# Low parts of the weights divided anew between VectorE and GpSimd, the row shift on GpSimd, and new orders on five engines

## What is computed

```python
x = x + 0.5 * ffn(layernorm(x))
x = x + attention(layernorm(x))
x = x + 0.5 * ffn(layernorm(x))

def ffn(x):                    # w_gate, w_up: 1024 x 256; w_down: 256 x 1024
    return (silu(x @ w_gate.T) * (x @ w_up.T)) @ w_down.T

def attention(x):
    x = x / max(norm(x), 1e-12) * 16 * gamma
    q, k, v = split(x @ w_qkv)           # then rotary positions on q and k
    p = softmax(mask(q @ k.T / 8))
    return (p @ v) @ w_out
```

## Time and profile before

| | us |
|---|---|
| median of three runs | 587.42 |
| the profiled execution | 586.27 |
| its span, first to last instruction | 584.4 |
| TensorE busy in the span | 561.9 (96%) |
| VectorE, ScalarE, GpSimd busy | 432.6, 379.5, 361.0 |

### The profile page before, as it was taken

How to read it: one execution, slowest core, us unless ns; L and a number is a source line. 1 busy time by engine, 2 the same in 40 slices (tenths; PEclk the granted TensorE clock), 3 DMA queues, 4 the chain that set the end, 5 groups by cost and what they waited for, 6 DMA issues and landing times.

```text
span 584.4 us, 13692 instructions
## 1 busy us (share of the span) xinstructions
PE 561.9 (96%) x4364; PEld 532.6 (91%) x4364; DVE 432.6 (74%) x1295; ACT 379.5 (65%) x1013; POOL 361.0 (62%) x344
## 2 busy tenths in 40 slices
PE   7788999999999999999999999999999999999997
PEld 3777999999999999999999999999999999789997
DVE  3687987769767795868867697777868698698533
ACT  4445892589736895379925897369934897379422
POOL 0556572887649765695838875597737877445322
PEclk9799999999999999999999999999999999999999
DMA  7340000350006200270004400080003500000001
GB/s 220 117 130 2 2 2 20 90 129 1 20 18 165 50 18 0 60 174 0 18 18 114 101 18 0 18 197 19 18 18 74 141 0 0 18 1 2 2 1 37
DMA packets 28090, 29.70 MB, mean 51 GB/s; under 512 B 2976, under 2 KB 25888, under 8 KB 28064
## 3 DMA queue, kind: packets, MB, share of 16 engines
q1 hardware_dynamic: 28064, 29.37, 19.3%
HBM read 8.39 MB, written 2.10 MB: 18 GB/s over the span
## 4 chain that ended last, share of the span: by engine, by line
PE 69%; DVE 9%; issue 8%; SPq 5%; POOL 4%; ACT 3%; DMA 2%; POOLq 0%; DVEq 0%; ACTq 0%
PE bank L958 44%; PE bank L967 9%; PE bank L1092 5%; PE bank L1062 5%; SPq L292 3%; PE bank L1087 3%; PE bank L1058 2%; SPq L281 2%; PE bank L1054 1%; DVE rope_s L722 1%; POOL probs L404 1%; DVE hid L839 1%; POOL hid_lo L413 1%; DMA eye_sb<-in_eye 1%; ACT xn L483 1%
## 5 line engine op out<-in xcount | busy, mean ns | idle before, releaser
L404 POOL TENSOR_TENSOR probs<-probs,inv_sum 128x512 f32<-128x512 f32 (+1 forms) x64 | 93.9, 1470 | 56.0 <-DVE inv_sum L807 55.9
L547 ACT ACTIVATE probs<-probs,neg_max 128x128 f32<-128x128 f32 (+1 forms) x256 | 113.2, 450 | 4.1 <-DVE neg_max L797 3.9
L413 POOL TENSOR_TENSOR hid_lo<-hid,hid_hi 128x512 fp32r<-128x512 f32 x64 | 83.0, 1301 | 36.2 <-ACT hid_hi L587 35.0
L958 PE MATMUL bank<-xf_t_hi,gate_hi 128*128 128x256 f32 x256 | 75.5, 295 | 7.1 <-DVE gate_lo L650 3.7
L958 PE MATMUL bank<-down_hi,hid_hi 128*128 128x256 f32 x256 | 73.0, 285 | 1.6 <-POOL hid_lo L413 1.6
L958 PE MATMUL bank<-xf_t_hi,up_hi 128*128 128x256 f32 x256 | 72.2, 282 | 0.0
L958 PE MATMUL bank<-xf_t_hi,gate_lo 128*128 128x256 f32 x256 | 71.9, 281 | 0.0
L958 PE MATMUL bank<-xf_t_lo,gate_hi 128*128 128x256 f32 x256 | 71.9, 281 | 0.0
L958 PE MATMUL bank<-down_lo,hid_hi 128*128 128x256 f32 x256 | 71.8, 281 | 0.0
L958 PE MATMUL bank<-down_hi,hid_lo 128*128 128x256 f32 x256 | 71.7, 280 | 0.0
L958 PE MATMUL bank<-xf_t_hi,up_lo 128*128 128x256 f32 x256 | 71.3, 279 | 0.0
(11 more groups left out here) (141 smaller groups left out, 1832.3 us busy)
## 6 DMA issues: line engine op xcount, KB each, us to landing
q_t<-rotated SPq DMA_DIRECT2D x96, 128.0 KB, 2.7
k_t<-rotated_k SPq DMA_DIRECT2D x48, 128.0 KB, 2.7
x_in<-in_x SPq DMA_DIRECT2D x7, 256.0 KB, 2.7
out<-y_out SPq DMA_DIRECT2D x7, 256.0 KB, 2.1
probs<-in_w_qkv SPq DMA_DIRECT2D x4, 384.0 KB, 3.8
probs<-in_w_gate SPq DMA_DIRECT2D x2, 512.0 KB, 7.0
probs<-in_w_up SPq DMA_DIRECT2D x2, 512.0 KB, 7.9
probs<-in_w_down SPq DMA_DIRECT2D x2, 512.0 KB, 4.2
```

The source lines that it names most:

```text
L404: nc.gpsimd.tensor_tensor(part, part, inv_sum[:, slot].unsqueeze(2).broadcast_to([P, GROUP, keys]), ALU.mult).then_inc(p_done, 1)
L413: nc.gpsimd.tensor_tensor(hid_lo[:, slot].rearrange("p c n -> p (c n)"), hid[:, slot], hid_hi[:, slot].rearrange("p c n -> p (c n)").bitca ...
L547: last = nc.scalar.activation(part, part, ACT.Exp, bias=neg_max[:, slot, g:g + 1], scale=-1.0, accum_out=row_sum[:, slot, g:g + 1])
L958: last = nc.tensor.matmul(dst, a[x], b[y], start=start and i == 0, stop=stop and i == 2, skip_group_check=shared)
```

## The change

- The low parts of pieces 4 and 5 (down) move from GpSimd to VectorE; GpSimd keeps pieces 10 and 11 (output).
- The shift of the rows for the feed-forward blocks moves from VectorE to GpSimd, straight behind the power (`shift_rows`). For attention it stays on VectorE (`unit_shift`). `statistics` now waits for the shift before (`shift_set`) ahead of the three small instructions that overwrite what the shift reads.
- The pieces of query, key and value come in the order of their columns. `eye` is loaded ahead of the weights, `gamma` and the second example behind piece 4.
- TensorE's waits for weights move into `gate`, `up`, `down`, `qkv` and `projection` (`weight`). Its six `keep_warm` calls stand together, and the wait for `eye` behind them.
- All lists of calls are new, and one pair of transfers of SyncE in the loop changes places.

The diff, cut to its core (in the lists, lines that are left out differ too):

```diff
-                   for k in range(KC) for i in (0, width)]
+                   for i in (0, width) for k in range(KC)]
...
-        ON_POOL = [i for i in range(W_GATE_UP, W_ALL) if pieces[i][2] is None]
+        ON_POOL = [10, 11]
...
             sp.dma_start(x2[:], rows(x, 0)).then_inc(x0_loaded, 16)
+            sp.dma_start(eye_sb[:], eye).then_inc(eye_in, 16)
             for i, (src, _, _) in enumerate(pieces):
                 if i >= 4:
                     sp.wait_ge(*lo_done(i - 4))
                 sp.dma_start(stage(i), src).then_inc(w_in[i % 4], 16)
-                if i == 0:
-                    sp.dma_start(eye_sb[:], eye).then_inc(eye_in, 16)
-                if i == W_GATE_UP - 1:
+                if i == 4:
                     sp.dma_start(gamma_sb[:], gamma).then_inc(gamma_in, 16)
                     sp.dma_start(x_in[:], rows(x, 1)).then_inc(x_loaded, 16)
...
-                k_restack(0), q_restack(0), k_restack(1), q_restack(1), k_restack(2), q_restack(2), k_restack(3)
+                k_restack(0), q_restack(0), k_restack(1), q_restack(1), q_restack(2), k_restack(2), k_restack(3)
...
-            def powers():
+            def shift_rows():
+
+                pool.wait_ge(ln_pow, turn.at(ln_pow, c["LN"] + 1))
+                nc.gpsimd.tensor_tensor(shift[:], less_mean[:], power_out[:, 0], ALU.mult).then_inc(shift_set, 1)
+
+            def powers(unit=False):
 
                 pool.wait_ge(ln_var, turn.at(ln_var, c["LN"] + 1))
                 if c["LN"]:
                     pool.wait_ge(xn_ready, turn.at(xn_ready, c["LN"]))
                 nc.gpsimd.tensor_tensor(power_out[:], power_in[:], exponent[:], ALU.pow
                                         ).then_inc(ln_pow, 1)
+                if not unit:
+                    shift_rows()
                 c["LN"] += 1
 
...
-            powers(), hidden_lo(), split_lo(4), powers(), split_lo(5), hidden_lo(), hidden_lo(), hidden_lo()
-            powers(), split_lo(10), split_lo(11), row_add("opening", 0, 0), row_add("opening", 0, 1)
-            row_add("opening", 0, 2), row_add("opening", 1, 0), row_add("opening", 1, 1), hidden_lo(), hidden_lo()
+            powers(), hidden_lo(), powers(), hidden_lo(), hidden_lo(), hidden_lo(), powers(True), split_lo(10)
+            hidden_lo(), row_add("opening", 0, 0), row_add("opening", 0, 1), row_add("opening", 0, 2)
+            row_add("opening", 1, 0), row_add("opening", 1, 1), split_lo(11), hidden_lo()
...
-                powers(), rope_add(0), rope_add(1), rope_add(2), powers(), rope_lo(2), rope_add(3), rope_add(4)
-                hidden_lo(), rope_lo(3), low_mask(), low_mask(), rope_lo(4), hidden_lo(), low_mask(), low_mask()
...
+                powers(), rope_add(0), rope_add(1), rope_add(2), rope_lo(2), powers(), rope_add(3), rope_add(4)
+                hidden_lo(), rope_lo(3), low_mask(), low_mask(), hidden_lo(), rope_lo(4), low_mask(), low_mask()
...
+                outputs_lo(), hidden_lo(), powers(True), normalise(), hidden_lo(), outputs_lo(), hidden_lo()
...
-            powers(), row_add("ending", 0, 0), row_add("ending", 0, 1), row_add("ending", 0, 2)
+            row_add("ending", 0, 0), row_add("ending", 0, 1), powers(), row_add("ending", 0, 2)
...
-            split_hi(0), normal_rows(x2), x_hi(xf_t), split_hi(1), split_hi(2), tanh(), split_hi(3), hidden_hi()
-            tanh(), split_hi(4), tanh(), hidden_hi(), split_hi(5), normal_rows(x_in), split_hi(6), split_hi(7)
-            tanh(), hidden_hi(), hidden_hi(), x_hi(xf_t), split_hi(8), split_hi(9), tanh(), split_hi(10), keep_x1()
-            normal_rows(x1_next, True), tanh(), x_hi(xa_t), split_hi(11), q_hi(0, 0), hidden_hi(), q_hi(0, 1)
...
+            normal_rows(x2), x_hi(xf_t), split_hi(0), split_hi(1), tanh(), split_hi(2), split_hi(3), hidden_hi()
+            tanh(), tanh(), split_hi(4), hidden_hi(), split_hi(5), split_hi(6), tanh(), hidden_hi()
+            normal_rows(x_in), hidden_hi(), split_hi(7), split_hi(8), x_hi(xf_t), split_hi(9), tanh(), split_hi(10)
+            keep_x1(), normal_rows(x1_next, True), tanh(), x_hi(xa_t), hidden_hi(), hidden_hi(), q_hi(0, 0)
+            q_hi(0, 1), k_hi(0), split_hi(11), q_hi(1, 1), q_hi(1, 0), exps(), exps(), tanh(), k_hi(1), exps()
...
-                rope_hi(3), hidden_hi(), tanh(), low_copy(), rope_hi(4), low_copy(), hidden_hi(), normal_rows(x2)
-                exps(), low_copy(), hidden_hi(), low_copy(), tanh(), x_hi(xf_t), low_copy(), exps(), low_copy()
+                hidden_hi(), rope_hi(3), rope_hi(4), hidden_hi(), tanh(), low_copy(), low_copy(), exps(), low_copy()
+                low_copy(), hidden_hi(), normal_rows(x2), tanh(), exps(), x_hi(xf_t), low_copy(), low_copy()
...
+                hidden_hi(), outputs_hi(), p_hi(7, 1), hidden_hi(), normal_rows(x1_next, True), small_half(6)
+                p_hi(7, 0), x_hi(xa_t), small_half(7), outputs_hi()
...
                 settle(last)
+                if c["LN"]:
+
+                    dve.wait_ge(shift_set, turn.at(shift_set, c["LN"]))
+                c["LN"] += 1
                 nc.vector.tensor_scalar(power_in[:, 0], mean_var[:, :, 1], EPS, None, ALU.add)
...
-            def row_shift(unit=False):
-
-                dve.wait_ge(ln_pow, turn.at(ln_pow, c["LN"] + 1))
+            def unit_shift():
+
+                dve.wait_ge(ln_pow, turn.at(ln_pow, c["LN"]))
                 rstd = power_out[:, 0]
...
-                nc.vector.tensor_tensor(shift[:], less_mean[:], rstd, ALU.mult).then_inc(shift_set, 1)
-                c["LN"] += 1
...
+                nc.vector.tensor_tensor(shift[:], less_mean[:], factor[:], ALU.mult).then_inc(shift_set, 1)
...
-            statistics(x2), row_shift(), split_lo(0), x_lo(xf_t), split_lo(1), gate_product(), up_product()
-            gate_product(), up_product(), split_lo(2), first_statistics(), split_lo(3), row_shift(), gate_product()
-            up_product(), split_lo(6), split_lo(7), gate_product(), up_product(), x_lo(xf_t), split_lo(8)
-            split_lo(9), ffn_residual(x1_next, x2), attention_statistics(), gate_product(), row_shift(True)
...
+            statistics(x2), x_lo(xf_t), split_lo(0), split_lo(1), gate_product(), up_product(), split_lo(2)
+            split_lo(3), gate_product(), up_product(), first_statistics(), gate_product(), up_product(), split_lo(4)
+            split_lo(5), split_lo(6), gate_product(), up_product(), split_lo(7), split_lo(8), x_lo(xf_t)
+            ffn_residual(x1_next, x2), attention_statistics(), gate_product(), split_lo(9), unit_shift()
...
-                first_statistics(), rope_products(0), rope_products(1), row_shift(), second_statistics(x2)
-                rope_products(2), x_lo(xf_t), rope_lo(0), rope_lo(1), rope_products(3), gate_product(), up_product()
-                rope_products(4), gate_product(), up_product(), gate_product(), row_shift(), up_product()
...
+                first_statistics(), rope_products(0), rope_products(1), rope_products(2), second_statistics(x2)
+                x_lo(xf_t), rope_lo(0), rope_lo(1), rope_products(3), gate_product(), up_product(), rope_products(4)
+                gate_product(), up_product(), gate_product(), mask_max(0), mask_max(1), up_product(), value_halves()
...
+                if c["Q"] in (0, 1):
+                    weight(W_QKV - KC * (2 - c["Q"]) + 1)
...
+                if c["Y"] == 0:
+                    weight(W_ALL - 1)
...
+            def weight(i):
+
+                semaphore, count = lo_done(i)
+                pe.wait_ge(semaphore, turn.at(semaphore, count))
+
             def gate():
                 pe.wait_ge(t_lo, turn.at(t_lo, c["ff"]))
+                if c["F"] < PAIRS and c["F"] % 2 == 0:
+                    weight(c["F"])
                 pe.wait_ge(gate_used, turn.at(gate_used, c["F"]))
                 hidden_product(gate_w, G_BANK).then_inc(g_ready, 1)
 
...
-            keep_warm(3)
-            pe.wait_ge(eye_in, turn.at(eye_in, 16))
-            keep_warm(3), x_transposes("ff")
-            pe.wait_ge(w_lo, turn.at(w_lo, 1))
-            gate()
-            pe.wait_ge(w_lo, turn.at(w_lo, 2))
-            up(), gate(), up()
-            pe.wait_ge(w_lo, turn.at(w_lo, 3))
-            gate()
-            pe.wait_ge(w_lo_pool, turn.at(w_lo_pool, 1))
-            down()
-            pe.wait_ge(w_lo, turn.at(w_lo, 4))
-            up(), gate(), up(), down(), x_transposes("ff")
-            pe.wait_ge(w_lo_pool, turn.at(w_lo_pool, 2))
-            down(), down(), gate(), up(), gate(), x_transposes("xa"), up()
-            pe.wait_ge(w_lo, turn.at(w_lo, 8))
-            qkv(0, 0), qkv(0, 1), qkv(0, 2), qkv(1, 0), q_transposes("opening", 0, 0), q_transposes("opening", 0, 1)
-            qkv(1, 1), qkv(1, 2), q_transposes("opening", 0, 2), gate()
...
+            keep_warm(6), x_transposes("ff"), gate(), up(), gate(), up(), gate(), up(), gate(), up(), down(), down()
```

(19 more changed lines are left out.)

157 lines of the change are left out of this document (75 added, 82 removed).

## The result

The kernel after takes 608.73 us (median of four runs, 605.61 to 610.53), the kernel before 587.25 us on the same chip: a ratio of 1.0365 with an interval of 1.034 to 1.0389. The forecast was 582.8 us with a range up to 586.5: it missed in sign and in size. The profiled execution took 608.41 us, its span is 606.6 us against 584.4. Both signs of being wrong that the prediction names came: the opening ends later instead of earlier, and TensorE stands for 15.3 us in the loop, where more than 6 was to be the sign.

A forecast was written before the change was run, and what follows sets the result against it. The loop was taken as bound by TensorE's own work, with 4.7 us at most to give back. Terms summed to -4.6 us, 581.7 on the profiled execution; 1.15 to the median gives 582.8 us, range 579.0 to 586.5.

The forecast's parts named there:

- Both signs of being wrong: Stated tests of failure: the opening gains less than 1 us, or TensorE stands more than 6 us in the loop.
- Orders of the loop: Loop: `x_hi` behind `exps` adds a wait of 0.2 us a turn, +1.2 us over six turns.
- First attention rows: Opening: the unit shift again stands beside GpSimd's output low part, so the 3.1 us wait stays: 0.
- The slower rival: Loop: late maxima put all of `exps` between transposes and gate, 1.4 us a turn, 590.0 us; chance 0.08.
- First gate: Opening: the first weights' high part now stands behind `x_hi`, so this gate starts at 12.7, not 12.22: +0.5 us.
- Third gate: Opening: this gate starts at 20.9 instead of 22.17 if VectorE stands for a hidden low part: -1.3 us.
- Clock: Opening, behind the stall ahead of the third gate: the stretch at half clock goes, -2.1 us.
- the second rival: Opening: half clock falls from the first gate on instead, losing 2.1 us as before, 584.9 us; chance 0.17.
- Down's low parts: Opening: two splits of 1.23 us moved to VectorE, mostly covered by TensorE's work: +0.3 us.
- Seam: Opening: next rows' transposes move behind three of four projections, leaving one to cover `x_hi` and `x_lo`: +0.4 us.
- Shift on GpSimd: Feed-forward rows come 1.3 us earlier, removing TensorE's wait: -2.4 us over six turns, -0.4 us in the ending.
- Ending: Fourth qkv product ahead of the first query transposes covers most of a 1.1 us wait: -0.8 us; earlier rows: -0.4.

The follow-up runs named there:

- e8: Kernel after, lists untouched, with the attention shift cut from five VectorE instructions to one; 586.50 us.
- e1: Kernel after with the attention shift made by one GpSimd instruction behind the power, the five VectorE instructions gone; 583.91 us.
- e5: Kernel after with the attention shift as one GpSimd instruction and the loop's lists of before; 581.94 us.
- e11: e5 with the lists of before from the first query product to the loop; 580.30 us.
- e9: e5 with the second gate product moved ahead of the low part of up's second half in VectorE's list; 580.41 us.
- e7: Kernel before with only the feed-forward shift moved to GpSimd, straight behind the power; 585.59 us.
- e6: Kernel before, its lists and weight division untouched, with all three shifts of a turn on GpSimd; 581.66 us.
- e12: e5 with the changes of e9, e10 and e11 together; 578.42 us.
- e4: Kernel after with the loop's last two hidden low parts and the output low part between them cut to 64 of 512 columns; 588.01 us.
- e2: Kernel after with the loop's attention transposes, and ScalarE's copy of them, moved back to their old later place; 613.36 us.
- e3: Kernel after with all five lists of the loop as before; feed-forward shift stays on GpSimd, attention chain on VectorE; 585.35 us.
- e10: e5 with five more warming calls between the first transposes and the first gate; 580.88 us.

## Why the prediction was wrong

**The step that failed** is "Orders of the loop. One place I price". I priced `x_hi` behind `exps` at +1.2 us and everything else in the new lists at nothing. That place cost nothing: no such wait is in the trace, and with the chain gone the new lists cost 0.9 to 2.5 us over six turns in all (e8 and e1 against e5). What I did not price was that VectorE's list sets the attention chain ahead of the last low parts of the probabilities, where GpSimd works through `hidden_lo`, `outputs_lo`, `hidden_lo` without a pause. I had the mechanism in hand: the earlier trace rows show a small instruction of this chain taking 2.35 us beside GpSimd, and I used it for the opening ("First attention rows", 0). I looked for meetings where the trace of before had them, and the old loop has none: its chain stood behind the last low parts and took 0.93 us each turn. The check that was missing is to lay VectorE's and GpSimd's new lists side by side at each chain of dependent instructions, and to count one meeting for each link that can have one (here three of five), not one for the chain.

**The slower rival** had the right sign for the wrong place, and its price of 1.4 us a turn was short of 2.0 of standing and, in four turns, 1.7 of half clock. That a stand of 2 us in the loop brings half clock was not in the forecast at all; it makes 7.0 of the 18.9 us.

**First gate**, +0.5: it started at 13.20, +1.0, since the last warming matmul ended later than I took it to. In the seven other kernels with the same lists up to there (e1 to e5, e8, e11) it lies between 11.65 and 12.51, and in e9 at 13.01, so this term is within what single executions differ by.

**Third gate**, -1.3: 22.57 against 22.17, no gain. I had put the meeting at the low part of gate, which took 1.22 us; it fell on that of up (2.32), and the gate product stood behind it. With that exchanged (e9) the opening gains 1.5.

**Clock**, -2.1: the stretch behind the third gate is at full clock, but that was luck: the seven other kernels named under the first gate all show half clock there, somewhere between 21.4 and 26.6 us. The kernel after has two other stretches in the opening, one in the first gates and ups, from 14.3 to 17.7, which is the second rival, and one from 45.0 to 48.4, behind the stand of 3.40 us for the first attention rows, which no rival has. Before, TensorE lost 2.6 us by half clock from 22.17 to 27.3; now it loses 3.2 up to the first query product. Its stands up to there are 11.2 us instead of 11.5, so third gate and clock together came to nothing, not to -3.4.

**Down's low parts**, +0.3: the wait for the `x_lo` of the second example is there (0.70 us at 36.50), and the two for hidden low parts have shrunk from 0.93 to 0.15 us in all; the move was not tried by itself. **Seam**, +0.4: no wait appears for it, but the lists of the second half of the opening cost 1.4 us (e11). I had priced one place of them.

**First attention rows**, 0: right for the wait (3.40 us against 3.1), but the half clock behind it is new. It is the largest gain that the change left lying: in e1 the wait is 0.36.

**Shift on GpSimd**, -2.4 in the loop: the wait for feed-forward rows went as I said, but only 1.3 us of it arrives (e7), as the rope products are late next. I had called the rope additions covered, and did not ask what the earlier transposes would wait for.

**Ending**, -0.8 and -0.4: e1 and e5 have 77.4 and 77.5 us from its first product to the end, before had 78.3: -0.9. In the kernel after it is 78.7, at a mean clock of 0.98 over the ending.

## What to carry to other kernels

A chain of small dependent VectorE instructions whose operands lie in the State Buffer can lose the rest of a GpSimd instruction at each of several links (here at three of five, 2.4 us together); before its place in an order is changed, look at what GpSimd runs there. If GpSimd already makes the number that the chain starts from, let it make the end of the chain too: one edit of that kind gave e6 its 1.0% with nothing reordered. And price an order by every place where two engines meet, not by the one that catches the eye; a stand of TensorE of 2 us can cost nearly twice its length.

## What the hardware showed beyond what I expected

- Of the five small instructions, the reciprocal never stood: 166 to 167 ns in all eight, also at 159.57, 0.10 us into a GpSimd instruction, while the product behind it took 982 ns beside the same one. The three that stood are two products with both inputs in the State Buffer, and a maximum with a constant, which has only one (1236 ns). The fifth, the product of the shift, came when GpSimd was through; as the only instruction, in e8, it stood too (684 ns). VectorE's instructions that read a bank, such as `p_odd_lo` with 0.69 us, took the same beside GpSimd as alone. The Trainium skill, SBUF — State Buffer, "SBUF: two separate sides", lists as instructions that need the shared port pair those with two inputs in the State Buffer and those in a two-port mode, and has the loser wait for the whole instruction of the other. The trace agrees as far as the products and the bank reads go; that the maximum ran in such a mode and the reciprocal didn't would fit, but no run here shows the mode. Who started first is not to be read from a start alone: in the meeting of the earlier trace rows it was the first of the two VectorE instructions, begun 0.07 us ahead of GpSimd, that took 2.18 us instead of 1.0, and the VectorE instruction ahead of it ended only at 29.69, behind GpSimd's start at 29.67.
- GpSimd can be the one that stands. In e5 its shift of the first attention rows took 0.90 us instead of 0.19: it began at 39.69, 0.17 us behind a low part of the weights on VectorE (39.52, 1.01 us, as long as alone), and ended 0.06 us behind it. e1 and e9 to e12 have the same single meeting among their 24 shifts, e6 has none.
- With the GpSimd instructions cut to an eighth of their columns (e4) the maximum still met one of them and lost 0.1 us, and the two products met none. Shorter instructions shorten a meeting and also make it rarer; the runs don't part the two.
- A stand of TensorE of 2.0 us was followed by some 3.4 us at half clock in four of six turns; in the first and the fourth turn the same stand was not. In the opening, the stand for the first attention rows was not followed by one before (3.1 us) and in e2 (3.4 us), but it was in e7 (3.1 us) and in e3, e4 and the kernel after (3.4 us each). Stands of 0.9 and 0.8 us in the ending of e12 were, and one of 1.7 us in e10 was not. What decides was not tried.
- The scatter of a kernel goes with these stretches. Of the 18 executions of the kernel before beside e1 to e4, the two with a mean clock of 0.997 took 585.2 and 585.3 us, and the three with 0.988 took 588.3 to 588.6. So a difference of 1 us between two profiles is to be read only after looking for them.
